# Mamba scan layers rebuilt: B·(delta·u) formed by TensorE with diagonals, states times C on GpSimd, states summed by TensorE

## What is computed

```python
xc, z = split(x @ W_in.T)                     # 1024 channels each
u = silu(causal_conv4(xc) + b_c)
dt, B, C = split(u @ W_x.T)                   # 32, 16, 16 columns
delta = softplus(dt @ W_dt.T + b_dt)
h[t] = exp(delta[t] * A) * h[t-1] + delta[t] * u[t] * B[t]     # per channel, 16 states
y[t] = sum_n h[t, :, n] * C[t, n] + u[t] * D
out = (y * silu(z)) @ W_out.T
```

## Time and profile before

| | |
|---|---|
| median of 3 runs | 9133.01 us (9124.58 to 9134.03) |
| profiled execution, first to last instruction | 9119.7 us (of this execution the profile gives no other time) |
| TensorE, products | busy 7422.6 us, 81% |
| TensorE, weight loads | busy 3968.2 us, 44% |
| VectorE | busy 8449.9 us, 93% |
| ScalarE | busy 5597.6 us, 61% |
| GpSimd | busy 6002.9 us, 66% |
| DMA | mean 61 GB/s |

### The profile page before, as it was taken

The page is one execution under the profiler, slowest core; times in us unless marked ns, Lnnn a source line. Parts: engine busy times, 40 slices in busy tenths (PEclk is TensorE's granted clock), DMA queues, the critical chain, the costliest instruction groups (busy, mean ns, idle before and its releaser), DMA issues. The chain is left out here.

```text
span 9119.7 us, 124311 instructions
## 1 busy us (share of the span) xinstructions
PE 7422.6 (81%) x29640; PEld 3968.2 (44%) x29640; DVE 8449.9 (93%) x9986; ACT 5597.6 (61%) x9722; POOL 6002.9 (66%) x4680
## 2 busy tenths in 40 slices
PE   5788888888888888888888888888888888867886
PEld 3444444444444444444444444444444444444753
DVE  2999999999999999999999999999999999996716
ACT  5666666666666666666666666666666666643515
POOL 0777777777777777777777777777777777772203
PEclk7899999999999999999999999999999999968888
DMA  5111111111111111111111111111111111113434
GB/s 191 43 48 47 47 41 48 48 48 44 48 48 47 46 47 43 46 59 58 57 45 48 48 48 47 47 47 44 49 48 49 45 49 49 44 41 119 184 118 147
DMA packets 221783, 552.86 MB, mean 61 GB/s; under 512 B 24496, under 2 KB 24752, under 8 KB 200048
## 3 DMA queue, kind: packets, MB, share of 16 engines
q1 hardware_dynamic: 194672, 459.30, 15.8%
q10 hardware_dynamic: 26368, 84.95, 2.3%
HBM read 442.44 MB, written 101.71 MB: 60 GB/s over the span
## 5 line engine op out<-in xcount | busy, mean ns | idle before, releaser
L769 POOL TENSOR_TENSOR bu<-w,b_rep 128x512 f32<-128x512 f32 x4096 | 5210.2, 1276 | 2178.9 <-DVE h L804 2171.6
L804 DVE TENSOR_TENSOR_SCAN h<-decay,h_last,bu 128x512 f32<-128x512 f32 x3840 | 4882.7, 1272 | 28.5 <-POOL bu L769 19.9
L644 ACT ACTIVATE decay<-delta,neg_a 128x512 f32<-128x512 f32 x4096 | 2802.9, 689 | 2839.7 <-DVE h L804 2822.1
L438 PE MATMUL turn<-ident_m,h 128*128 128x128 f32 x16384 | 2698.5, 290 | 1321.7 <-DVE h L804 726.7
L438 PEld LDWEIGHTS turn<-ident_m,h 128*128 128x128 f32 x16384 | 1984.6, 147 | 3918.2 <-issue 2041.9
L815 DVE SCALAR_TENSOR_TENSOR acc<-turn,c_now,acc 128x512 f32<-128x512 f32 x3840 | 2777.3, 723 | 5.3 <-PE turn L438 4.0
L382 PE MATMUL proj<-x_conv,w_in 128*128 128x512 f32 x2048 | 1088.1, 624 | 54.7 <-issue 29.2
L382 PE MATMUL proj<-zy,w_out 128*128 128x512 f32 x2048 | 1050.0, 607 | 2.5 <-issue 2.5
L382 PE MATMUL proj<-conv_in,conv_diag 128*128 128x512 f32 x2048 | 1040.1, 602 | 9.6 <-ACT halo L561 9.6
L382 PE MATMUL proj<-x_gate,w_in 128*128 128x512 f32 x2048 | 1023.1, 594 | 0.0
L804 DVE TENSOR_TENSOR_SCAN h<-decay,zeros_m,bu 128x512 f32<-128x512 f32 x256 | 325.3, 1272 | 125.2 <-POOL bu L769 125.1
(11 more groups left out here) (167 smaller groups left out, 5480.4 us busy)
## 6 DMA issues: line engine op xcount, KB each, us to landing
b_rep<-b_rows SPq DMA_DIRECT2D x1024, 256.0 KB, 3.2
x_conv<-xt SPq DMA_DIRECT2D x32, 1024.0 KB, 6.2
x_gate<-xt SPq DMA_DIRECT2D x32, 1024.0 KB, 6.4
xt<-stage ACTq DMA_DIRECT2D x128, 256.0 KB, 2.4
x_n<-in_x_dram SPq DMA_DIRECT2D x16, 1024.0 KB, 5.2
xt<-xt_n ACTq DMA_DIRECT2D x16, 1024.0 KB, 4.1
x_l<-in_x_dram SPq DMA_DIRECT2D x16, 1024.0 KB, 5.7
mt_l<-xt SPq DMA_DIRECT2D x16, 1024.0 KB, 5.4
```

The source lines that it names most:

```text
L438: mm = pe.transpose(turn[:, tn.n % RING, b * P:(b + 1) * P], h[:, k % 2, b, j * P:(j + 1) * P], ident[:])
L644: act.activation(decay[:, b, :], delta[:, blk, :], ACT.Exp, scale=neg_a[:, n, blk:blk + 1]).then_inc(decay_set, 1)
L769: pool.tensor_tensor(bu[:, b, :], w[:, blk, :], b_rep[:, k % 4, :], ALU.mult).then_inc(bu_set, 1)
L804: dve.tensor_tensor_scan(h[:, k % 2, b, :], decay[:, b, :], bu[:, b, :], start, ALU.mult, ALU.add).then_inc(scanned, 1)
```

## The change

In the Mamba layers only:

- **B (delta u).** GpSimd makes w = delta u in `tmp`; TensorE turns it once per block (`turn_w`) and ScalarE copies it to `w_t`, with time on the partitions. For each chunk and state GpSimd makes four 128x128 diagonals of B (`diag_of`, from the turned x_proj output `b_t`). In each slot TensorE (`fill`) makes four products of 128 columns, w_t times the diagonal, which gives B delta u back with channels on the partitions, in one of two PSUM banks `bu`.
- **The scan** stays on VectorE, reads the decay from SBUF and `bu` from PSUM, and writes into a ring of 8 states.
- **C and the sum.** GpSimd multiplies two states at a time, 128x1024, by a spread row of C (`product`). TensorE (`sum_pair`) adds each into `y` in PSUM by a product of 512 columns with the identity, and starts each sum with diag(D) times u. `add_state`, `turn_states`, `turn_y`, `sum_y`, `skip` and `acc` go.
- **Softplus** is done per block: the bias is a row of the weights, ScalarE takes abs, exp, ln, and VectorE (`delta_of`) makes max(x, 0) plus the logarithm.
- **Order.** `ORDER` and `timetable` are new: products are placed at 1.4 per slot with lags of their own, ScalarE takes tiles 4 slots behind, and some slots at the end of a chunk have none. `set_d` makes the diagonals of D. SP loads rows of C, with the gate's input at group 3 (8 before) and the next conv input at 25 (20 before); the bias of delta comes by a gathered load of 1024 single numbers at each layer. ScalarE preloads the table set for exp and ln behind each silu.

```diff
+ORDER = ([("conv_half", 0, 0), ("conv_half", 1, 0), ("delta", 4, 6), ("out", 0, 7), ("delta", 5, 0), ("out", 1, 0),
...
+RATE = 1.4
+TAKE_LAG, TAPS_LEAD, DELTA_LAG, W_LAG, TURN_W_LAG, X_PROJ_LAG, XDBL_LAG, SILU_Z_LAG = 4, 2, 5, 6, 9, 5, 3, 9
+SUM_LAG = 4
...
-        def turn_states(tn, G, k, j):
...
-            for b in range(HB):
-                mm = pe.transpose(turn[:, tn.n % RING, b * P:(b + 1) * P], h[:, k % 2, b, j * P:(j + 1) * P], ident[:])
-            mm.then_inc(turn_full, 1)
...
+        def fill(G, kind, s):
...
+            pe.wait_ge(scanned, G * SLOTS_BODY + (s - 1 + C_SCAN))
...
+            for j in range(J):
+                mm = pe.matmul(bu[:, s % 2, j * P:(j + 1) * P], w_t[:, blk, j, :], diag[:, n, j, :], start=True, stop=True)
+            mm.then_inc(bu_full, 1)
+
+        def sum_pair(G, s):
+
+            pe.wait_ge(prod_set, G * PAIRS + (s // 2 + 1 + C_PROD))
+            k, b0 = divmod(s, HB)
+            hf, n = divmod(k, STATES)
+            if n == 0:
+                for b in (b0, b0 + 1):
...
+                    pe.matmul(y[:, b, :], d_diag[:, b, :], u[:, hf * HB + b, :], start=True, stop=False).then_inc(skipped, 1)
+            for b in (b0, b0 + 1):
+                pe.matmul(y[:, b, :], ident[:], h[:, (s + b - b0) % (2 * HB), 0:T], start=False,
+                          stop=n == STATES - 1).then_inc(summed, 1)
...
+            for s in range(SLOTS_BODY):
+                if s + 1 < SLOTS_BODY:
+                    fill(G, kind, s + 1)
...
+                if s % 2 == 0 and s >= SUM_LAG:
+                    sum_pair(G, s - SUM_LAG)
...
     @block.gpsimd
...
-            pool.tensor_tensor(bu[:, b, :], w[:, blk, :], b_rep[:, k % 4, :], ALU.mult).then_inc(bu_set, 1)
...
+        def diag_of(X, n):
...
+            pool.tensor_tensor(diag[:, n, :, :], b_t[:, :, n].unsqueeze(2).to_broadcast([P, J, P]),
+                               ident[:].unsqueeze(1).to_broadcast([P, J, P]), ALU.mult).then_inc(diag_set, 1)
+
+        def product(G, p):
...
+            pool.wait_ge(scanned, G * SLOTS_BODY + (s + 2 + C_SCAN))
+            pool.tensor_tensor(h[:, at:at + 2, 0:T], h[:, at:at + 2, 1:1 + T],
+                               c_rep[:, k % 4, :].unsqueeze(1).to_broadcast([P, 2, T]), ALU.mult).then_inc(prod_set, 1)
...
     @block.vector
...
-            dve.tensor_tensor_scan(h[:, k % 2, b, :], decay[:, b, :], bu[:, b, :], start, ALU.mult, ALU.add).then_inc(scanned, 1)
-
-        def add_state(tn, k, j):
...
-                ins = dve.scalar_tensor_tensor(acc[:, hf, j, :], turn[:, tn.n % RING, :], scalar, acc[:, hf, j, :],
-                                               ALU.mult, ALU.add)
...
+            dve.tensor_tensor_scan(h[:, at, 1:1 + T], decay[:, b, :], bu[:, s % 2, :], start, ALU.mult, ALU.add).then_inc(scanned, 1)
+
+        def delta_of(X, b, place):
...
+            dve.scalar_tensor_tensor(delta[:, b, :], proj[:, place % RING, :], 0.0, tmp[:, b % HB, :], ALU.max, ALU.add).then_inc(delta_set, 1)
```

More of the change, by code:

```diff
@@ L53 @@
 RING = 2
[L55 to L75, removed]
@@ L89, in timetable @@
+DELTA_KINDS = ("delta", "delta_next")
 def timetable():
[L92 to L101, removed]
@@ L102, in timetable @@
-    p = 0
-    for kind, x in ORDER:
-        slots = [slot_of[p + q] for q in range(PRODUCTS[kind])]
+    at, ends, end_of = 0.0, [], {}
+    work, take = [[] for _ in range(SLOTS_BODY)], [[] for _ in range(2 * SLOTS_BODY)]
+    delta_at, w_at = [[] for _ in range(2 * SLOTS_BODY)], [[] for _ in range(2 * PAIRS)]
+    for i, (kind, x, earliest) in enumerate(ORDER):
+        at = max(at, earliest)
+        if i >= RING and ORDER[i - RING][0] in DELTA_KINDS:
+            at = max(at, ends[i - RING] + DELTA_LAG + 1)
+        if kind in ("turn_w", "turn_w_next"):
+            at = max(at, end_of["delta" + kind[6:], x] + TURN_W_LAG)
+        if kind == "x_proj":
+            at = max(at, end_of["conv", NB - 1] + X_PROJ_LAG)
+        if kind == "turn_b":
+            at = max(at, end_of["x_proj", 0] + XDBL_LAG)
+        slots = [int(at + q / RATE) for q in range(PRODUCTS[kind])]
+        at += PRODUCTS[kind] / RATE
@@ new lines, in tiles @@
+def tiles(first, last):
+    place, acts, n, freed = {}, {}, 0, 0
+    for i, (kind, _, _) in enumerate(ORDER):
+        if first and kind in NOT_FIRST or last and kind in NOT_LAST:
+            continue
+        place[i], acts[i] = n, freed
+        n, freed = n + 1, freed + (kind not in DELTA_KINDS)
+    return place, acts, n, freed
+PROJ_TILES, PROJ_FREED = tiles(False, False)[2:]
+PROJ_FIRST, FREED_FIRST = tiles(True, False)[2:]
+PROJ_PROLOGUE, FREED_PROLOGUE = 2 * NB + 1 + 1 + HB + HB, 2 * NB + 1 + 1 + HB
@@ L154, in __init__, with has @@
         self.layer_next = layer + self.leaves
+        self.place, self.acts, self.n_tiles, self.n_freed = tiles(self.first, self.last)
+    def has(self, what):
+        return not (self.first and what in NOT_FIRST or self.last and what in NOT_LAST)
 def all_chunks(eng, run):
@@ L344, in _ @@
         load_xproj_weights(0)
+        sp.wait_ge(zeros_set, 4)
         load_delta_weights(0)
@@ new lines, in _, with prologue_bank @@
+        before = Kind(0)
+        def prologue_bank(n, acts):
+            pe.wait_ge(proj_done, max(0, acts - (RING - 1)) + C_PROJ)
+            return proj[:, n % RING, :]
+        X, n = 0, 0
+        for b in range(0, NB, 2):
+            for half in (b, b + 1):
+                conv_half(prologue_bank(n, n), X, 0, half, (0, KD))
+                n += 1
+            for whole in (b, b + 1):
+                conv(prologue_bank(n, n), X, whole, (0, TAPS))
+                n += 1
+        x_proj(prologue_bank(n, n), X, 0, (0, NB))
@@ L672, in take_tiles @@
-        def take_tiles(pj, G, position, kind):
-            for what, x in TAKE[position]:
-                if kind.first and what in NOT_FIRST or kind.last and what in NOT_LAST:
-                    continue
-                if what == "delta":
-                    delta_proj(pj, G, kind.layer, x)
-                if what == "taps" and not kind.last:
-                    taps(kind.layer_next, x)
+            for half in (b, b + 1):
+                conv_half(first_tile(n), n + C_PROJ, X, half)
+                n += 1
@@ new lines, in _ @@
+            for whole in (b, b + 1):
+                conv(first_tile(n), X, whole)
+                n += 1
+        for hf in range(2):
+            silu_u(n + C_PROJ, hf)
+        set_d(0, 0, 0)
+        x_proj(first_tile(n), X)
+        n += 1
+        turn_b(first_tile(n), X)
+        n += 1
+        for b in range(HB):
+            delta_abs(first_tile(n), b)
+            n += 1
+            delta_exp(X, b)
+            delta_ln(X, b)
+        for b in range(HB):
+            turn_w(first_tile(n), b)
+            n += 1
@@ L700, in take_tiles @@
[L700 to L705 removed]
+                    silu_z(freed + 1, x)
         def body(G, kind):
[L708 to L710 removed]
             if kind.enters:
@@ new lines, in _ @@
+        for n in range(5):
+            diag_of(0, n)
+        for b in range(HB):
+            w_of(0, b)
+        def body(G, kind):
+            for p in range(PAIRS):
+                if not kind.first:
+                    for what, x in W_AT[PAIRS + p]:
+                        w_of(G - 1 + (what == "delta_next"), x)
+                for what, x in W_AT[p]:
+                    if kind.has(what):
+                        w_of(G + (what == "delta_next"), x)
+                for n in DIAG_LATE_AT.get(p, ()):
+                    diag_of(G, n)
+                if not kind.last:
+                    for n in DIAG_AT.get(p, ()):
+                        diag_of(G + 1, n)
+                product(G, p)
@@ new lines, in _ @@
+        for b in range(HB):
+            delta_of(0, b, 2 * NB + 2 + b)
+        def body(G, kind):
+            for s in range(SLOTS_BODY):
+                scan(G, kind, s)
+                for what, x, i in DELTA_AT[s]:
+                    if kind.has(what):
+                        delta_of(G + (what == "delta_next"), x, kind.place[i])
+                if s in HALF0_GATE_AT:
+                    gate_y(G, HALF0_GATE_AT.index(s))
+                if s in HALF1_GATE_AT and not kind.first:
+                    gate_y(G - 1, HB + HALF1_GATE_AT.index(s))
```

714 lines of the change are left out of this document (343 added, 371 removed).

## The result

The changed kernel takes 12,625.26 us (median of 4 runs, 12,620.65 to 12,630.04) against 9,130.42 us for the kernel before (median of 4): ratio 1.3828, 95% interval 1.3809 to 1.3848. It is 38% slower. Its profiled execution took 12,630.04 us, with a span of 12,627.3 us. The prediction started from 9,133 us for the kernel before, the median of three of these four runs.

A forecast was written before the change was run, and what follows sets the result against it. VectorE was taken to bound the kernel before, TensorE the changed one. 253 us to the first scan, 11,554 for the stage and 811 behind it give 12,618, plus 13 for the median: 12,631 us, range 12,300 to 13,400.

The forecast's parts named there:

- VectorE and GpSimd after: Scan stage of the changed kernel: VectorE 175 us a chunk instead of some 250, GpSimd 181 us.
- a sign for VectorE: Sign of a right forecast: VectorE near 5,600 us busy and waiting for TensorE's bu before its scans.
- The fill: TensorE, each slot: four 128-column products as 8 instructions of 0.112 us, 0.90 us in all.
- its two rivals: Fill runs' rivals: only columns and weights count, no change; or unhidden weight loads make half the fill, under 11,000 us.
- The sum: TensorE, each slot: one product of 512 columns with the identity, 0.86 us.
- A chunk: TensorE in the scan stage: 360 us a chunk, against 184 us by the same prices before.
- Waits: TensorE in the scan stage: nothing added for waits, up to 3% (354 us) for the upper bound.
- The clock: TensorE's granted clock in the stage: 0.99 taken, giving 11,554 us; 11,438 us at 1.00.
- The ends: Outside the stage: 253 us to the first scan, 811 us behind the stage, 13 us for the median over the span.
- The clock's rival: TensorE's clock sags to 0.83 with short products: stage 13,780 us, whole 14,860 us; 5 in 100.
- The rival with dear short products: Fills on TensorE: load and product don't overlap at 128 columns, 1.76 us a fill, 16,030 us; 4 in 100.
- The faster case: TensorE: identity and diagonal products at the transposes' price, 181 us a chunk, about 7,000 us; 3 in 100.

The follow-up runs named there:

- The gates on GpSimd: Kernel before with the 8 gates of a chunk moved from VectorE to GpSimd, one group later: 8,889.38 us, ratio 0.9736.
- the run with half of the product: Changed kernel with GpSimd multiplying only the first 256 steps of each state by C: 12,633.58 us.
- the transposes: Changed kernel with the four products of a fill replaced by four transposes of w, factor B left out: 10,931 us.
- the wide product: Changed kernel with one product of 512 columns for a fill, three of four weight blocks left out: 12,493.11 us.
- The nearest run: Changed kernel with fills as four transposes and sums over 256 columns, half of each sum left out: 9,427 us.
- the quarter sum: Changed kernel with fills as four transposes and sums over 128 columns, three quarters of each sum left out: 8,742 us.

## Why the prediction was right, step by step

- **What bounded the kernel before:** VectorE. The gates on GpSimd show it, since 8.1 us a chunk taken from it came off the time almost whole.
- **VectorE and GpSimd after:** 175 and 181 us a chunk were foretold; by the groups it is 163.6 + 10.7 = 174 and 139 + 17 + 10 = 166, as the product by C took 2.18 us (2.35 assumed) and a diagonal 1.05 (1.28 assumed). The 5,600 us named as a sign for VectorE are its work in the stage alone (5,557 by its four groups); the page's 5,996 include the other stages. For GpSimd the run with half of the product shows that its sum did not matter; that VectorE's did not is read from the 5,607 us that its scans idle.
- **The fill:** 0.90 us a slot foretold, 0.89 measured; its two rivals are settled by the transposes (0.44) and the wide product (0.86).
- **The sum:** 0.86 us foretold and measured; half of it is worth 1,647 us.
- **A chunk:** 360 us foretold at full clock. A full chunk takes 364.2; the 361.8 that the stage gives over 32 stands against 357 foretold, both without the first chunk's 76 products.
- **Waits:** none foretold, 64 us measured between 500 and 11,700 us (32 for a scan, 22 of issue, 10 for a bank of turned w).
- **The clock:** 0.99 taken, 1.00 granted. By that alone the stage would be 11,438 us; of the 140 us above, 64 are the waits, and the other 76, some 2.4 us a chunk, are pieces slightly dearer than priced, which were not told apart. The 0.99 covered most of the 140 by luck: 11,554 foretold, 11,578 measured. The dips of the kernel before were also misread as lying in one place of a chunk: besides the one shown in rows 9, the grant is 0.83 at 5,520 to 5,530 and at 5,540 to 5,550 us.
- **The ends:** first scan at 234.6 us, 18 earlier than the 253 foretold and below the lower end of that estimate (236), since the five diagonals (219.7 to 224.8 us on GpSimd) and the delta work ran side by side; 814.5 us behind the stage, 811 foretold. The 13 us added for the median over the span measured 3 in this kernel's own profiled run. These misses of 24, 3, -18 and -10 us nearly cancel, so that 12,631 came within 6 us of 12,625 is luck; the method's error is some tens of us.
- **The clock's rival** (0.83) did not come: short products mixed with long ones, without gaps, kept the full clock (1.00).
- **The rival with dear short products** was added up slightly wrong: 0.86 us more for each of 128 fills is 111 us a chunk, not 105, and 3,540 us, not 3,400. The fill measured 0.89 us, so nothing hangs on it.
- **The faster case** needed one-instruction products, and these were two. Its sum is also wrong: 62 us for the projections halves all 144 of them, though only the 32 taps are diagonal products; with these alone halved the chunk is 229 us and not 181, and the time near 8,400 us, not 7,000. The nearest run, with fills at 0.44 and sums at 0.43 us, took 9,427 us and was no faster than the kernel before; only the quarter sum fell below it (8,742 us). So fewer columns on TensorE do give the time back, but the turning point is below the 252 us that the rival names.

## What to carry to other kernels

Before work is moved to TensorE, count the columns of all its instructions, not of its calls: an f32 transpose was one instruction, an f32 product two, each streaming all columns, and a product with an identity or a diagonal cost as much as any other (0.86 us for 512 columns). Cutting the same columns into more instructions cost next to nothing here. Compare the new sum of that engine with the old pace of the bound engine; here 360 against 252 us decided the matter before any question of waits. When the two come near each other, add for waits: 246 us of work ran at 263 us a chunk, and 242 beside 250 at 265. Then look at the bound engine's small operations one by one, not by their mean, for one that an idle engine can take: eight gates a chunk gave 2.6%, where the whole rebuild lost 38%.

## What was not expected of the hardware

- **The clock and transposes.** The kernel before, with transposes, was granted 0.96 between 500 and 7,800 us. With the transposes of the states as ordinary products, and TensorE's busy time up from 6,073 to 6,972 us in that stretch, it was granted 1.00. With fills as transposes in the changed kernel and TensorE busy for 98% it was 0.99, and with a quarter of the sum besides 0.98, at a busy time (6,938 us) almost that of the run that was granted 1.00. The Trainium skill ("TensorE: Matmul & The Clock Gate", Part 4) says that transposes don't count as activity for the gate. These numbers agree in direction, the last pair at nearly the same busy time, but those two are different kernels. The grant was 4% below full in the kernel before, not half of it, and it was 1.00 between 4,085 and 4,125 us, where 81 of TensorE's 129 instructions were transposes.
- **Two SBUF operands on VectorE.** The same gate took 1.33 us where a GpSimd product ran beside its start, and 0.69 us where none did. The addition before it, with one operand in PSUM, took 0.67 us although such a product ran beside it (4,066.32 us).
- **GpSimd.** A product with one operand spread over two states took 2.18 us for 128x1024, against 2.35 for one of the same size with two full operands; with both operands spread 1.05 us for 128x512, against 1.28. The run with half of the product has the step between, 1.18 us for 128x512 with one operand spread. No run changed the operands alone.
